# Cross attention: the transposed weights stored block first, and the key unit ahead of the value unit in every step

## The reference

```python
q = (query @ Wq.T + bq).reshape(b, lq, HEADS, HEAD_DIM)
k = (key @ Wk.T + bk).reshape(b, lk, HEADS, HEAD_DIM)
v = (value @ Wv.T + bv).reshape(b, lk, HEADS, HEAD_DIM)
scores = jnp.einsum('bqhd,bkhd->bhqk', q * scale, k)
probs = jax.nn.softmax(scores, axis=-1)
attn = jnp.einsum('bhqk,bkhd->bqhd', probs, v).reshape(b, lq, HIDDEN)
```

## Time and profile before

| | |
|---|---|
| median of 3 runs | 2744.11 us |
| profiled execution, its own time | 2746.47 us |
| span of its trace | 2744.6 us |
| cross attention, from the first move to the last weighted sum | 615.2 to 2191 us |
| DMAs of the moves | 2048 of 96.0 KB |

### The profile page before, as it was taken

One profiled execution on the slowest core, in us unless ns is written; L12 is line 12 of the kernel. 1 busy time (PEld: TensorE's weight loads), 2 busy tenths in 40 slices (PEclk: granted clock), 3 DMA queues, 4 the chain that ended last, 5 costly groups with the idle time before them and its releaser, 6 DMA issues. The chain is left out here.

```text
span 2744.6 us, 56719 instructions
## 1 busy us (share of the span) xinstructions
PE 2526.0 (92%) x21216; PEld 2053.9 (75%) x21216; DVE 1531.6 (56%) x2593; ACT 1281.8 (47%) x2452; POOL 1343.8 (49%) x1185
## 2 busy tenths in 40 slices
PE   8999999979999999999999999999999569999998
PEld 7888857877777777777677777777767358988987
DVE  7555568826556556566566555665656433354352
ACT  3544542125556555565565555555656342212311
POOL 4666553225555556555565555655645223333332
PEclk9999979989999999999999999999999679999999
DMA  7554437537787777777777777777777661011010
GB/s 228 156 152 122 143 110 272 203 88 159 170 177 170 168 174 170 176 172 166 171 174 177 162 172 174 172 170 169 175 170 156 132 219 43 16 58 42 15 35 20
DMA packets 470208, 398.03 MB, mean 145 GB/s; under 512 B 140220, under 2 KB 415676, under 8 KB 469948
## 3 DMA queue, kind: packets, MB, share of 16 engines
q1 hardware_dynamic: 469948, 394.58, 58.5%
HBM read 140.66 MB, written 52.43 MB: 70 GB/s over the span
## 5 line engine op out<-in xcount | busy, mean ns | idle before, releaser
L1096 POOL TENSOR_SCALAR D_e<-D_e,D_inv 128x722 f32<-128x722 f32 x256 | 538.2, 2102 | 700.9 <-DVE D_inv L1185 700.9
L1179 DVE TENSOR_REDUCE D_neg_max<-D_ps_s 128x1 f32<-128x722 f32 x512 | 441.8, 904 | 591.8 <-PE D_ps_s L1253 591.5
L1146 ACT ACTIVATE D_e<-D_ps_s,D_neg_max 128x722 f32<-128x722 f32 x512 | 437.5, 860 | 177.1 <-DVE D_neg_max L1179 176.8
L1193 DVE STREAM_TRANSPOSE D_turned<-D_e 128x768 f32<-128x768 f32 x512 | 483.3, 961 | 1.4 <-POOL D_e L1096 1.3
L65 PE MATMUL D_ps_p<-D_ctx_high,cross_wk_high 128*128 128x362 f32 x1024 | 357.5, 349 | 45.7 <-ACT D_values L1141 34.0
L65 PE MATMUL D_ps_p<-D_ctx_low,cross_wk_high 128*128 128x362 f32 x1024 | 337.0, 329 | 0.0
L65 PE MATMUL D_ps_p<-D_ctx_high,cross_wk_low 128*128 128x362 f32 x1024 | 336.7, 329 | 0.0
L65 PE MATMUL D_ps_p<-cross_wv_high,D_ctx_high 128*128 128x512 f32 (+1 forms) x768 | 315.5, 411 | 1.1 <-ACT D_values L1141 1.1
L65 PE MATMUL D_ps_p<-cross_wv_low,D_ctx_high 128*128 128x512 f32 (+1 forms) x768 | 307.6, 401 | 0.0
L65 PE MATMUL D_ps_p<-cross_wv_high,D_ctx_low 128*128 128x512 f32 (+1 forms) x768 | 306.8, 399 | 0.0
L1133 ACT ACTIVATE D_keys<-D_ps_p,D_bk_c 128x362 f32<-128x362 f32 x256 | 144.0, 562 | 338.2 <-PE D_ps_p L65 338.2
(11 more groups left out here) (187 smaller groups left out, 5036.6 us busy)
## 6 DMA issues: line engine op xcount, KB each, us to landing
D_pT<-D_turned SPq DMA_DIRECT2D x2048, 96.0 KB, 2.3
D_craw<-in_ctxT SPq DMA_DIRECT2D x126, 361.0 KB, 4.0
D_qraw<-cross_q SPq DMA_DIRECT2D x64, 200.0 KB, 3.8
self_q<-A_q_out SPq DMA_DIRECT2D x10, 640.0 KB, 3.8
self_k<-A_k_out SPq DMA_DIRECT2D x10, 640.0 KB, 3.2
self_v<-A_v_out SPq DMA_DIRECT2D x25, 256.0 KB, 2.1
A_q<-self_q SPq DMA_DIRECT2D x32, 200.0 KB, 3.9
A_k<-self_k SPq DMA_DIRECT2D x32, 200.0 KB, 4.4
```

What stands on the lines that cost most here:

```text
L1096: pool.tensor_scalar(head, head, inv[:, 2 * (s % 2):2 * (s % 2) + 1], None, ALU.mult)\
L1146: act.activation(e[n // 2 % 2][:, n % 2, 0:S].rearrange("p (a b) -> p a b", a=2), both_banks(n), ACT.Exp, bias=neg_max[:, n % 4:n % 4 + 1] ...
L1179: dve.tensor_reduce(neg_max[:, n % 4:n % 4 + 1], both_banks(n), AX.XY, ALU.max, negate=True)\
L1193: dve.transpose(turned[quad % 2][:, 2 * (s % 2) + h, :, :].rearrange("p j (t r) -> p t j r", r=32), e[s % 2][:, h, :].rearrange("p (t j r) ...
```

## The change

The two tiles `turned` and `pT` get their block index ahead of their head index, `[P, BLOCKS, 4, RUN]`, and the three places that use them are turned round with them. The slice of one DMA of a move is then `[:, a, :, :]`: for each of its 32 rows the four heads lie side by side, 4 x 768 = 3072 B. Bytes, number of DMAs and waits stay. VectorE's transpose writes blocks j at a stride of 768 words instead of 192; TensorE reads its four runs of 25 columns at a stride of 768 words instead of 192.

The second part sorts the units of each step: `"k"` comes ahead of `"v"`. Only steps 2 and 3 of the eight change their order. The turns of the two PSUM banks, the counts of `u_done` and TensorE's order all follow from the sorted list. ScalarE's order of work within a step does not change.

```diff
@@ -951,8 +951,8 @@
-        turned = [sb(f"turned{i}", [P, 4, BLOCKS, RUN]) for i in range(2)]
-        pT = [sb(f"pT{i}", [P, 4, BLOCKS, RUN]) for i in range(2)]
+        turned = [sb(f"turned{i}", [P, BLOCKS, 4, RUN]) for i in range(2)]
+        pT = [sb(f"pT{i}", [P, BLOCKS, 4, RUN]) for i in range(2)]
@@ -997,6 +997,8 @@
+        for s in unit_at:
+            unit_at[s].sort()
         every_step = range(FIRST, STEPS + SUM_AFTER)
@@ -1054,8 +1056,8 @@
-                            sp.dma_start(pT[quad % 2][32 * j:32 * (j + 1), :, a, :],
-                                         turned[quad % 2][32 * a:32 * (a + 1), :, j, :]).then_inc(moved_sem(quad), 16)
+                            sp.dma_start(pT[quad % 2][32 * j:32 * (j + 1), a, :, :],
+                                         turned[quad % 2][32 * a:32 * (a + 1), j, :, :]).then_inc(moved_sem(quad), 16)
@@ -1190,7 +1192,7 @@
-                    dve.transpose(turned[quad % 2][:, 2 * (s % 2) + h, :, :].rearrange("p j (t r) -> p t j r", r=32),
+                    dve.transpose(turned[quad % 2][:, :, 2 * (s % 2) + h, :].rearrange("p j (t r) -> p t j r", r=32),
@@ -1267,7 +1269,7 @@
-                                             pT[quad % 2][:, j, :, 32 * i:32 * i + QB],
+                                             pT[quad % 2][:, :, j, 32 * i:32 * i + QB],
```

## The result

The changed kernel takes 2713.22 us (median of 4 runs, 2706.27 to 2718.46) beside 2742.86 us for the kernel before (4 runs). The ratio is 0.9885, 95% interval [0.9856, 0.9915]: the time falls by some 30 us, 1.15%, clear of the interval, where I had forecast 94. The direction is right, the size is off by a factor of three; 2713 lies inside my range of 2628 to 2722, near its upper end.

What follows compares the result with a forecast made beforehand. SP's DMA issuing was taken as the bound, at 49.2 us a batch. 31 x (49.2 - 46.2) = 93 us plus 2.4 us in the last batch gave 2650 us; 8-in-10 range 2628 to 2722.

Steps and rivals of the forecast that it cites:

- SP's issuing is the bound: In cross attention, SP's queue issues DMAs without a break, 48.85 us over a batch, and TensorE waits for it.
- SP is never waiting for the transposes: On SP's queue over a batch, each stretch of DMA issues begins where the one before ends.
- TensorE's floor of 45.6 us: TensorE's scores, sums, key and value units need 45.6 us of a 49.2 us cross attention batch.
- Runs: Merged runs make each move DMA's issue on SP 45 to 50 ns shorter, 3.2 us a batch.
- It says that SP is more likely below 46.0 than above: SP's single long issues, 3 to 4 us a batch, might shorten with fewer descriptors; none taken in the sum.
- Order: Sorting steps 2 and 3 removes step 4's 1.1 us key-unit stall, 34 us of TensorE; no gain while SP is the bound.
- Strides: VectorE's transpose and TensorE's read of `pT`, at strides of 768 instead of 192 words, cost nothing extra.
- Rival 1: DMA issue on SP costs the same: 2744, chance 0.10; with 0.02 us an issue saved: 2704, chance 0.11.

Runs made afterwards that it cites:

- split_act: Changed kernel with 2 of the 16 DMAs of each quad's move issued by ScalarE's queue, the other 14 by SP's; 2622.43 us.
- eight_moves: Changed kernel issuing only 8 of the 16 DMAs of a move from the third quad on, so the output differs; 2611.43 us.
- hbm_source: Changed kernel whose move DMAs read their runs from an HBM tensor instead of SBUF from the third quad on, so the output differs; 2616.04 us.
- order_only: Kernel before with only the units of each step sorted, key first, and the 768 B runs kept; 2750.52 us, ratio to before 1.0021.
- old_layout_split: split_act with the two tiles laid out as before, four runs of 768 B a row; 2625.52 us, ratio to before 0.9571.

## Why the prediction went wrong

*SP's issuing is the bound:* right. split_act, which moves 8 of 64 issues a batch to another queue and leaves their number and bytes as they are, brings the batch from 48.5 to 45.5 us, and so do eight_moves and hbm_source. "SP is never waiting for the transposes" was a little too strong: it waited 12.3 us in 13 waits, 0.4 us a batch.

*TensorE's floor of 45.6 us:* right to 0.1 us in three kernels.

*Runs, "the move has its extra dimension on both sides ... I take twice 22, some 45 to 50 ns":* this is the step that failed. The term is 15 ns, 607 to 592, by which the sum is 31 x 0.96 = 30 us instead of 31 x 3.2 = 99. None of the issues of L312 and L335 stands behind an SBUF to SBUF move (50 of these 57 come after a pause), and for a move that doesn't stand behind another one the estimate was even low (585 to 507). But 15 moves of 16 stand behind another move, where a second cost takes over: some 580 to 600 ns behind an SBUF to SBUF DMA, in each of the shapes tried, and for the store and the context loads too. The trace of before had two signs of it. In the earlier trace rows the median is 22 ns over the least, and of the 1910 issues behind another move only 31 take less than 600 ns. In the earlier trace rows the store behind a move takes 0.60 us, where the stores of L312 and L335 take 0.34 and 0.36. I priced an issue that stands behind no move and multiplied by the count of those that do.

*"It says that SP is more likely below 46.0 than above":* wrong. The long issues stayed, 100 for 106; they go with the instruction fetches, not with the number of descriptors. They cost some 2.8 us a batch, where I had read 3 to 4 off the stretches of the earlier trace rows.

*Order: nothing while SP is full, and its stall gone:* right in the mechanism, but for 7 us that it costs (order_only). Its worth once SP is free was mis-sized, 34 for 73 us, for the overlooked second stall.

*Strides cost nothing:* right; the transposes take 962 ns on average after, 961 before, and a batch at TensorE's floor takes 45.5 us with the new layout (split_act), 45.6 with the old one (old_layout_split).

*Rival 1 "if only part is saved (0.02 us an issue...)" 2704:* this is what came, at 0.015 us, with a chance of 0.11. The Trainium skill's rule (Perfetto Trace Analysis, What "DMA-bound" means), by which larger descriptors are what matters when the issuing sequencer's track is solid, is not borne out here: four times larger ones took 15 ns of 607. Its other rule (DMA: Bandwidth & Descriptors, Why small descriptors are slow (HBM only)), that SBUF to SBUF data doesn't suffer from short runs, agrees roughly: the landing went from 2.3 to 2.2 us.

## What to carry to other kernels

When a queue that issues DMAs is full, price an issue by what stands ahead of it; the median and the least of the source line can be two different costs. Count, and which queue, matter before shape: with the sorted order, moving 2 of 16 issues to a second queue gave 91 us more than merging four runs into one. It gave only 11 with the old order, where TensorE's stalls were the next bound. And when one resource is full, a fix to another shows nothing, or a little worse; judge it again after the full one is relieved, for the order here went from costing 7 us to saving 73.

## What the runs showed of the hardware

- An SBUF to SBUF DMA issued directly behind another takes 591 to 607 ns of SP's queue, with 32 or 128 rows, 1 or 4 runs a row, 48 or 96 KB. With HBM as the source of both: 421.
- The cost goes with the DMA ahead: the same store to HBM takes 586 ns behind a move from SBUF and 424 behind one from HBM.
- Where no move stands directly ahead the shape does count: 585 ns at the least for 32 rows of four runs, 507 for 32 rows of one, 464 for 128 rows of one.
- SP's issues are held up, by 0.8 to 0.9 us each at the mean, in step with instruction fetches: 97 fetches and 92 long issues, 63 and 59, in nearly the same stretch.
- Writes of 768 KB to HBM, and reads of 384 KB behind them, took 10.5 and 6.5 us to land while the DMA engines were at 0.90.
